# Layer 1's attention mixed tile by tile, with the values' weights multiplied by the output weights first

## The reference, cut to what matters

```
h = film(rmsnorm(x, norm1_w), cond, film1_w, film1_b)
Q = h @ q_w + q_b
K = h @ k_w + k_b
V = h @ v_w + v_b
scores = einsum('bnd,bmd->bnm', Q, K) * D ** (-0.5)
attn = softmax(scores, axis=-1)
out = einsum('bnm,bmd->bnd', attn, V)
x = x_in + (out @ proj_w + proj_b)
```

## Time and profile before

| what | value |
|---|---|
| median of 3 runs | 2066.84 us (2066.07 to 2077.7) |
| the profiled execution | 2061.89 us, of which the span is 2060.2 us |
| PE busy in the span | 1857.8 us, 90% |
| DVE, ACT, POOL busy | 1474.2, 1186.7 and 803.6 us |
| `layer1_qkv`, from 210.5 to 262.8 us | PE busy 46.78 of 52.30 us |
| the attention, from 262.8 us to 398.6 us | three kinds of stage work on PE, below |

### The profile page before, as it was taken

How to read it: one execution, slowest core, us unless ns; L and a number is a source line. 1 busy time by engine, 2 the same in 40 slices (tenths; PEclk the granted TensorE clock), 3 DMA queues, 4 the chain that set the end, 5 groups by cost and what they waited for, 6 DMA issues and landing times. The chain is left out here.

```text
span 2060.2 us, 37230 instructions
## 1 busy us (share of the span) xinstructions
PE 1857.8 (90%) x14290; PEld 1185.1 (58%) x14290; DVE 1474.2 (72%) x2534; ACT 1186.7 (58%) x2034; POOL 803.6 (39%) x726
## 2 busy tenths in 40 slices
PE   5988989898999999998989699999999999892786
PEld 3766577688533333335767455555555555582786
DVE  5656733564589898987878677777777777637794
ACT  3333333332228687885667677777777777623563
POOL 3356520074040302001556545544444444204477
PEclk8999999899959899999999899999999999995798
DMA  5000000200433211211568944454455564215452
GB/s 151 0 1 21 4 18 1 62 1 1 153 103 94 50 41 38 56 51 60 171 197 263 265 96 100 107 124 106 102 124 124 124 154 117 59 63 174 139 156 44
DMA packets 196833, 191.40 MB, mean 93 GB/s; under 512 B 64240, under 2 KB 155248, under 8 KB 196400
## 3 DMA queue, kind: packets, MB, share of 16 engines
q1 hardware_dynamic: 193584, 184.82, 33.4%
q0 software_dynamic: 3072, 4.20, 1.1%
HBM read 121.33 MB, written 67.37 MB: 92 GB/s over the span
## 5 line engine op out<-in xcount | busy, mean ns | idle before, releaser
L1583 POOL TENSOR_SCALAR l3h_prob<-l3h_prob,l3h_inv 128x1024 f32<-128x1024 f32 x256 | 287.4, 1123 | 319.1 <-DVE l3h_inv L1555 319.1
L1549 DVE TENSOR_REDUCE l3h_nmax<-l3h_score 128x1 f32<-128x1024 f32 x256 | 313.4, 1224 | 136.0 <-PE l3h_score L1492 135.8
L1782 DVE TENSOR_REDUCE l2h_nm<-l2h_rowb 128x1 f32<-128x1024 f32 x256 | 303.0, 1218 | 31.1 <-PE l2h_rowb L1714 30.6
L1832 ACT ACTIVATE l2h_pT<-l2h_score 128x512 f32<-128x512 f32 x512 | 273.8, 597 | 67.8 <-PE l2h_score L1730 50.6
L1573 ACT ACTIVATE l3h_prob<-l3h_score,l3h_nmax 128x1024 f32<-128x1024 f32 x256 | 285.8, 1116 | 37.8 <-DVE l3h_nmax L1549 2.7
L1515 PE MATMUL l3h_out<-l3h_pT,l3h_vs 128*64 128x512 f32 x1024 | 274.4, 617 | 0.0
L1541 ACT ACTIVATE l3h_pT<-l3h_ring 128x512 f32<-128x512 f32 x256 | 152.8, 597 | 103.1 <-PE l3h_ring L1503 102.7
L1503 PEld LDWEIGHTS l3h_ring<-ident,l3h_prob 64*128 64x128 f32 x4096 | 172.9, 138 | 35.6 <-issue 7.8
L1539 DVE COPY l3h_pT<-l3h_ring 128x512 f32<-128x512 f32 x256 | 172.0, 672 | 2.0 <-PE l3h_ring L1503 2.0
L1503 PE MATMUL l3h_ring<-ident,l3h_prob 64*128 64x64 f32 x4096 | 169.2, 222 | 2.6 <-DVE l3h_pT L1539 2.3
L1744 PE MATMUL l2h_out<-l2h_pT,l2h_vs 128*32 128x256 f32 (+1 forms) x1792 | 164.9, 443 | 0.0
(11 more groups left out here) (468 smaller groups left out, 4299.4 us busy)
## 6 DMA issues: line engine op xcount, KB each, us to landing
q3first<-l_q SPq DMA_DIRECT2D x64, 256.0 KB, 5.1
l3h_Q<-l_q SPq DMA_DIRECT2D x64, 256.0 KB, 5.0
l_q<-l3qkv_hi SPq DMA_DIRECT2D x16, 512.0 KB, 5.1
l_q<-l3qkv_lo SPq DMA_DIRECT2D x16, 512.0 KB, 4.2
l_k<-l3qkv_hi SPq DMA_DIRECT2D x16, 512.0 KB, 4.3
l_k<-l3qkv_lo SPq DMA_DIRECT2D x16, 512.0 KB, 3.4
k3first<-l_k SPq DMA_DIRECT2D x64, 128.0 KB, 5.2
l3h_vs<-l_v SPq DMA_DIRECT2D x32, 256.0 KB, 3.1
```

Of the source, the lines that this page charges most:

```text
L1549: dve.tensor_reduce(self.nmax[:, t % 4:t % 4 + 1], self.score[t % 2][:, :], AX.X, ALU.max, negate=True).then_inc(self.maxes, 1)
L1583: pool.tensor_scalar(self.prob[:, q, :], self.prob[:, q, :], self.inv[:, q:q + 1], self.vscale, ALU.mult, ALU.mult).then_inc(self.scaled, 1)
L1782: dve.tensor_reduce(self.nm[:, mr % 2, at:at + 1], self.rowb[h][:, :], AX.X, ALU.max, negate=True).then_inc(self.maxes, 1)
L1832: act.activation(self.pT[:, g % 4, h, c * C:(c + 1) * C], self.score[v % 3][:, :], ACT.Exp).then_inc(self.exps, 1)
```

## The change

- The output weights are loaded with layer 0's last loads into `carry` at 3072 to 3584 (`l1_pw`), and the values' weights come in already transposed (`vwT`; the array is turned on the host when it is handed in). The load of `wp` at the attention's start goes.
- `layer1_qkv` begins with 4 float32 matmuls that make `v_w @ proj_w` in bank 6, which ACT copies to a tile `wv`. The bias `v_b` comes in as columns; ACT spreads it over 128 columns, 2 float32 matmuls multiply it by the output weights, and ACT copies the row to `bv`. V is made as before, with these weights and this bias.
- In the attention `mix` works on one tile of queries: the turned probabilities are the weights and 256 features of the values move, 8 tiles of keys times 3 passes, 24 matmuls of 256 columns. The result has the tokens in partitions and is added to `X` at once, from one of two output banks. `project`, `oT` and ACT's copies of it go. `pT` is four tiles deep where it was two groups of four.
- PE's order in iteration `t` is: scores of `t`, transposes of `t - 1`, mix of `t - 2`. DVE adds tile `t - 3` in its iteration `t`.

The diff, cut to its core:

```
-            for n in ("qw", "kw", "vw"):
+            for n in ("qw", "kw", "vwT", "pw"):
...
-            sp.wait_ge(ahead, 16 * 5)
+            sp.wait_ge(ahead, 16 * 6)
...
-            sp.dma_start(bv[:, :], rows(w["vb"])).then_inc(loaded, 16)
+            sp.dma_start(bvc[:, :], columns(w["vb"]), allow_slow_non_contiguous=True).then_inc(loaded, 16)
...
+            for k in range(KF):
+                act.activation(bvr[:, k, :], g["ident"][:, :], ACT.Identity, bias=bvc[:, k:k + 1], scale=0.0).then_inc(bvx, 1)
+            act.wait_ge(wvs, 1)
+            act.activation(wv[:, :, :], bank[6][:, :], ACT.Copy).then_inc(wvd, 1)
...
+                if c == 0:
+                    act.wait_ge(bvs, 1)
+                    act.activation(bv[:, :], bank[7][:, 0:D], ACT.Copy).then_inc(bvd, 1)
...
             nt.pe_turn(pe, 0)
+            for m in range(KF):
+                for k in range(KF):
+                    mm = pe.matmul(bank[6][:, m * D:(m + 1) * D], wvT[:, k, m * P:(m + 1) * P], wp[:, k, :],
+                                   start=k == 0, stop=k == KF - 1)
+            mm.then_inc(wvs, 1)
...
+                if c == 0:
+                    pe.wait_ge(bvx, KF)
+                    for k in range(KF):
+                        mm = pe.matmul(bank[7][:, 0:D], bvr[:, k, :], wp[:, k, :], start=k == 0, stop=k == KF - 1)
+                    mm.then_inc(bvs, 1)
+                    pe.wait_ge(wvd, 1)
                 for t in range(TC):
+                    if c == 0 and t == 2:
+                        pe.wait_ge(bvd, 1)
...
-        pT = [s.sb(f"pT_{n}", [P, 2, TB, C], F32R) for n in ("hi", "lo")]
+        pT = [s.sb(f"pT_{n}", [P, 4, TB, P], F32R) for n in ("hi", "lo")]
...
-            sp.dma_start(wp[:, :, :], w["pw"].rearrange("(k p) n -> p k n", p=P)).then_inc(loaded, 16)
...
+            def mix(t):
+                pe.wait_ge(emptied, 2 * (t + 1))
+                if t >= 2:
+                    pe.wait_ge(added, t - 1)
+                for k in range(TB):
+                    for i, (x, y) in enumerate(PASSES):
+                        mm = pe.matmul(ob[t % 2][:, 0:D], pT[x][:, t % 4, k, :], vp[y][:, t // TB * TB + k, :],
+                                       start=k == 0 and i == 0, stop=k == TB - 1 and i == 2)
+                mm.then_inc(outs, 1)
+
+            for t in range(T + 2):
...
-                if t >= 1:
+                if 1 <= t <= T:
                     turn(t - 1)
-                    if t % TC == 0:
-                        mix(t // TC - 1)
-                        project(t // TC - 1)
+                if t >= 2:
+                    mix(t - 2)
...
+            def residual(t):
+                if t == 0:
                     dve.wait_ge(xbs, T)
...
+                dve.reciprocal(inv[:, t:t + 1], total[:, t:t + 1]).then_inc(inverse, 1)
+                dve.wait_ge(outs, t + 1)
+                dve.wait_ge(inverse, t + 1)
+                dve.scalar_tensor_tensor(X[:, t, :], ob[t % 2][:, 0:D], inv[:, t:t + 1], X[:, t, :],
+                                         ALU.mult, ALU.add).then_inc(added, 1)
+
+            for t in range(T + 3):
...
-                if t >= 1:
+                if 1 <= t <= T:
                     empty(t - 1)
...
+                if t >= 3:
+                    residual(t - 3)
+                if T - 4 < t < T:
+                    dve.wait_ge(added, (t - T + 4) * TC)
+                    nt.dve_stats(dve, t - T + 3)
+                if t == T:
+                    nt.dve_norm(dve, 0)
...
             def high(t):
+                if t >= 4:
+                    act.wait_ge(outs, t - 3)
...
-                if t >= 1 and t % TC == 0:
-                    gr = t // TC - 1
-                    if gr >= 1:
-                        act.wait_ge(filled, (gr + 1) * TC * 2 + gr * 2)
-                    for m in range(KF):
-                        act.wait_ge(outs, gr * KF + m + 1)
-                        act.activation(oT[:, m, :], ob[m][:, :], ACT.Copy).then_inc(outc, 1)
+            for c in range(3):
+                nt.act_root(act, c)
```

More of the change, by code:

```diff
@@ L1067, in layer1_attention @@
         ring = [s.ps(f"ring{i}") for i in range(2)]
-        ob = [s.ps(f"out{i}") for i in range(KF)]
-        (loaded, xbs, scores, maxes, exps, filled, his, emptied, outs, outc, inverse) = (s.sem(n) for n in (
+        ob = [s.ps(f"out{i}") for i in range(2)]
+        (loaded, xbs, scores, maxes, exps, filled, his, emptied, outs, added, inverse) = (s.sem(n) for n in (
             "loaded", "bias_added", "scores", "maxes", "exps", "ring_filled", "turned_hi", "ring_emptied", "out_sum",
-            "out_copied", "inverse"))
+            "residual_added", "inverse"))
         ahead = s.sem("mlp_weights")
@@ L1098, in turn @@
                 for half in range(2):
[L1099 to L1100 removed]
+                    use = 2 * t + half
+                    if use >= 2:
+                        pe.wait_ge(emptied, use - 1)
                     for i in range(TC):
[L1102 removed]
+                        mm = pe.transpose(ring[half][:, i * P:(i + 1) * P],
                                           prob[:, t % 2, (half * TC + i) * P:(half * TC + i + 1) * P], ident[:, :])
@@ L1104, in turn @@
                     mm.then_inc(filled, 1)
[L1105 to L1109, removed]
-                if gr >= 1:
-                    pe.wait_ge(outc, gr * KF)
-                for m in range(KF):
[L1113 to L1131, removed]
@@ L1157, in empty @@
                     dve.wait_ge(his, 2 * t + half + 1)
-                    dve.tensor_tensor(place(1, t, half), ring[use[0] % 2][:, :].rearrange("p (k q) -> p k q", k=TC),
+                    dve.tensor_tensor(place(1, t, half), ring[half][:, :].rearrange("p (k q) -> p k q", k=TC),
                                       place(0, t, half).bitcast(F32), ALU.subtract).then_inc(emptied, 1)
-                    use[0] += 1
-            def residual(gr):
-                if gr == 0:
+            def residual(t):
+                if t == 0:
                     dve.wait_ge(xbs, T)
[L1165 to L1173, removed]
-            for t in range(T + 1):
+                dve.reciprocal(inv[:, t:t + 1], total[:, t:t + 1]).then_inc(inverse, 1)
[4 more added lines that the diff above has]
+            for t in range(T + 3):
                 if t < T:
@@ L1195, in high @@
             def high(t):
+                if t >= 4:
+                    act.wait_ge(outs, t - 3)
                 for half in range(2):
-                    use = 2 * (t + t // TC) + half
-                    act.wait_ge(filled, use + 1)
-                    if t % TC == 0 and half == 0 and t >= 2 * TC:
-                        act.wait_ge(outs, (t // TC - 1) * KF)
-                    act.activation(place(0, t, half), ring[use % 2][:, :].rearrange("p (k q) -> p k q", k=TC),
+                    act.wait_ge(filled, 2 * t + half + 1)
+                    act.activation(place(0, t, half), ring[half][:, :].rearrange("p (k q) -> p k q", k=TC),
                                    ACT.Copy).then_inc(his, 1)
```

43 lines of the change are left out of this document (14 added, 29 removed), and 2 rows, old and new, of the table views.

## The result

The changed kernel takes 2034.28 us (median of 4 runs, 2020.51 to 2039.57) where the kernel before takes 2066.45 beside it (4 runs): ratio 0.9844, 95% interval 0.9803 to 0.9885. The forecast was 2039.7 us, a ratio of 0.987. The profiled execution took 2030.35 us (span 2028.6) against 2061.89 (2060.2): 31.5 us less, where the sum said 27.1.

A forecast was written before the change was run, and what follows sets the result against it. PE was taken to bound the attention. 28.9 us less there and 1.8 more in `layer1_qkv` gave 27.1 less, a median of 2066.84 - 27.1 = 2039.7 us, range 2031 to 2052.

The forecast's parts named there:

- the sum: Whole kernel: 28.9 us less in the attention, 1.8 more in `layer1_qkv`, together 27.1 us less.
- The period: Attention, from one tile's maximum to the next: 3.63 us of scores and transposes plus 2.88 of mix, 6.5 us.
- The row of the same form: MLP's line 1323, same shape and passes, matmuls 0.120 us apart: taken as the new mix's rate, 2.88 us a tile.
- The rule of the Trainium skill: Mix's weight loads, if not hidden: 384 loads add about 41 us, about 2081; rival "the loads show", chance 0.04.
- Nobody makes PE wait: Attention: the saving of 28.9 us rests on PE waiting for nobody; rival, a wait in each tile, 2064, chance 0.09.
- 3 us of room at each link: Attention: 3 us of slack at each link between PE and the other engines, against a wait in each tile.
- The 0.1 us of handover: Attention's end, between PE's last matmul and DVE's last sum: 0.1 us, an estimate.
- the 0.2 before ACT's copies: Attention, before ACT empties the ring's halves: 0.2 us of handover by estimate, in the exponentials' 3.1 us.
- The attention: From tile 2's scores to DVE's last sum: 98.6 us, ending at 369.4 instead of 398.31, 28.9 us less.
- The term by term check: Attention's saving by pieces (project, copy waits, other waits, low clock, less longer mix): 25.8 us, kept as lower bound.
- `layer1_qkv`: Stage before the attention, with 12 added PE instructions: 1.8 us more, bounds 1.5 and 3.3.
- the stages behind are unchanged: MLP and later stages, behind the attention: taken as unchanged; the prediction would be wrong if they moved.

The follow-up runs named there:

- split128: The changed kernel with each 256-column matmul of the mix cut into two of 128 columns; attention 147.2 us, 2076.37 us in all.
- no_lag: The changed kernel with each tile's mix right behind its own transposes, without the one tile of delay; attention 137.6 us, 2055.0 us in all.
- short_project: The kernel before with 2 instead of 8 float32 matmuls in each `project`; attention 126.8 us, 2049.26 us in all.
- no_prep: The changed kernel without the product of values' and output weights and without the spread bias; attention 107.3 us, 2037.91 us in all.
- The later profile of the same kernel: The changed kernel again without edit, five rounds against the kernel before: 2029.07 us (6 runs) against 2058.82, ratio 0.9864.
- wide: The changed kernel with both passes over the high probabilities in one 512-column matmul; 2040.72 us (4 runs) against 2059.87 for the kernel before, ratio 0.9898.

## Why the prediction was right

The mechanism and its size hold; the sign and the range too. Point by point:

- **The period.** 6.5 us forecast, 6.49 measured, with matmuls 0.120 us apart. The row of the same form carried this. From the scores of tile 2 to the last sum the trace has 371.60 - 273.19 = 98.4 us, the sum 98.6. The rule of the Trainium skill (TensorE: Matmul & The Clock Gate, Part 3: Packing small matmuls), that loads overlap matmuls only in another row group, would have made each mix 2.6 us longer, an estimate (the prediction's 41 us over 16 tiles). The trace doesn't agree: the loads use all rows and are hidden. By the Trainium skill (TensorE: Matmul & The Clock Gate, LDWEIGHTS) a load of 128 columns takes 107 ns, worked out from its formula; the rows show 191 to 192 ns from a load's start to its end, but pairs of load and matmul 0.112 us apart in `split128`. That loads set this distance fits the 107 ns, and no run here proves it.
- **Nobody makes PE wait.** No such row in the stage. The prediction had 3 us of room at each link; in the trace it is 3.7, 4.0 and 4.7. `no_lag` shows what the one tile of delay is worth: 30 us. The 0.1 us of handover that the sum took by estimate before the last sum is 371.12 - (370.80 + 0.28) = 0.04; the 0.2 before ACT's copies changes no term.
- **The attention.** -28.9 forecast, -28.3 measured. From the first maximum to the last sum it is 371.60 - 269.82 = 101.8 against 398.31 - 267.40 = 130.9, 29.1 less; 0.8 us were given back before it, at the start, where the first scores ran at the low clock throughout. `short_project`, with the kernel before's code up to there, needs 5.50 us for this start as well, so the change is not needed for it.
- **The term by term check.** It gave 25.8 and left 3.1 as the drain and handover at each full stop, on argument alone. `no_lag` measures this at 0.26 us for each stop for DVE; eight stops would be 2.1 of the 3.1, if the stops for ACT's copy cost the same, which no run shows.
- **`layer1_qkv`.** +1.8 forecast, +1.3 measured. This term of the sum was mis-sized, and what came lies below its lower bound of 1.5. The 12 instructions took 3.11 + 0.86 = 3.97 us, inside the 2.7 to 4.5; but the bound took off only the filled wait, where the second transposes gave back 0.85 and Q and K 0.79 as well, since they no longer ran at the low clock. And the 1.3 is itself partly chance: `no_prep` and `short_project` show the stage without the preparation 1.0 us longer than the trace of the kernel before does, so that the preparation costs 0.3 to 1.3 us, not 1.8.
- **The step that failed** is the last one: that the stages behind are unchanged. Their instructions are, their time was not: 4.9 us less at a clock of 0.94 against 0.93. Without it the execution would have been 26.7 us shorter, against a sum of 27.1. The later profile of the same kernel has 1659.9 for this rest, `no_lag` 1653.1, `wide` 1665.3, `no_prep` 1666.6, and `short_project`, without the change, 1658.3: it varies by 13 us among kernels with the same code there, on both sides of the kernel before's 1661.9. The piece of layer 2's heads above, 59.2 us before and 56.1 behind the change, takes 62.1 us at a clock of 0.56 both in `split128`, which has the change, and in `short_project`, which has not. So the change does not decide it; what does stays open.
- **Luck.** That 26.7 and 27.1 agree so closely is partly chance. The trace of the kernel before was about 1.0 us faster in `layer1_qkv` and 0.9 us faster at the attention's first scores than `short_project` with the same code; against that neighbour the change would have gained about 28.6 us up to the last sum.

The forecast of the medians, 27.1 us less, lies inside both intervals (23.8 to 40.7 us in the first comparison, 18.9 to 36.9 in the second).

## What to carry to other kernels

Where one engine bounds a stage and waits for the result of its own last step, order the work so that the step which needs the result runs one tile later: here the same instructions took 137.6 us without the delay and 107.2 with it. It needs buffers for one tile more and a bounding engine that has other work meanwhile. Turning a product round, so that 256 columns move over each load instead of 512, cost little here: 24 x 0.120 = 2.88 us a tile against 12 x 0.227 = 2.72. With 128 columns it cost 5.38. And it may take a whole later product away, when two constant matrices can be multiplied once. Read a stage by its own length from the trace, and from more than one trace: several microseconds of the total, and one or two of a stage, are the granted clock's.

## What the hardware showed that was not expected

- Float32r matmuls, each with its own load of 128 columns, stood 0.112 us apart at 128 moving columns (`split128`), 0.120 at 256 and 0.227 at 512: halving 256 columns saved next to nothing.
- Executions of one kernel differ by 16 to 20 us for 0.01 of mean granted clock (for example 2022.77 us at 0.941, 2040.71 at 0.930).
- At the start of the attention, behind PE's wait of 4.28 us, the trace of the kernel before shows five scores at the high level before the low one; every other trace of this study has the low level from the first score on, 0.8 to 0.9 us more.
- Removing 4 us of TensorE's work, 3.1 of them at or near the low level, from `layer1_qkv` made the stage 0.3 us shorter: TensorE waited 0.96 us again, and the work behind ran slower.
- The same 276 instructions of TensorE at the start of layer 2's heads took 56.1, 59.2 or 62.1 us at a granted clock of 0.67, 0.60 and 0.56, and not by which kernel it was.
